# Filter pass: attention output matmuls in four row groups, column differences on GpSimd

## What is computed

```python
def _conv_att2(x, kg_w1, kg_b1, kg_w2, kg_b2, lk_filter, fus_w, fus_b):
    f_att, f_idt = (x[:, :ATT], x[:, ATT:])
    ...
    out_dk = jax.vmap(dyn)(f_att, ker)
    out_lk = _conv(f_att, lk_filter, pad=LK // 2)
    out = jnp.concatenate([out_lk + out_dk, f_idt], axis=1)
    return _conv1x1(out, fus_w, fus_b)
...
x = x + _L0_conv_ref(_gn(x), ...)
x = x + _L1_conv_ref(_gn(x), ...)
```

## Time and profile before

| | us |
|---|---|
| median of 3 runs | 2881.2 (2880.36 to 2883.96) |
| profiled execution, span from first to last instruction | 2878.9 |
| PE matmul busy | 2655.4 (92%) |
| VectorE busy | 2144.7 (74%) |
| ScalarE busy | 1055.2 (37%) |
| GpSimd busy | 639.2 (22%) |

### The profile page before, as it was taken

One profiled execution on the slowest core, in us unless ns is written; L12 is line 12 of the kernel. 1 busy time (PEld: TensorE's weight loads), 2 busy tenths in 40 slices (PEclk: granted clock), 3 DMA queues, 4 the chain that ended last, 5 costly groups with the idle time before them and its releaser, 6 DMA issues. The chain is left out here.

```text
span 2878.9 us, 38918 instructions
## 1 busy us (share of the span) xinstructions
PE 2655.4 (92%) x12262; PEld 2134.0 (74%) x12262; DVE 2144.7 (74%) x2968; ACT 1055.2 (37%) x1641; POOL 639.2 (22%) x663
## 2 busy tenths in 40 slices
PE   5999999979998899999998799999967999999998
PEld 4777777758887688888886677777745777777776
DVE  5444444554554888888887799999878999999998
ACT  0211111111110788988997322222103233233232
POOL 6544444312221444444443100000001000000000
PEclk9999999978896899999999899999978999999999
DMA  7222222210000887787775133334442343333332
GB/s 149 68 77 75 75 76 75 54 34 6 13 13 18 196 224 218 219 220 216 221 214 166 62 134 135 135 135 155 156 155 108 97 122 92 98 118 93 98 119 59
DMA packets 288703, 338.04 MB, mean 117 GB/s; under 512 B 24817, under 2 KB 243825, under 8 KB 274289
## 3 DMA queue, kind: packets, MB, share of 16 engines
q1 hardware_dynamic: 280736, 334.74, 39.6%
q10 hardware_dynamic: 7888, 2.29, 0.5%
HBM read 211.60 MB, written 122.62 MB: 116 GB/s over the span
## 5 line engine op out<-in xcount | busy, mean ns | idle before, releaser
L168 PE MATMUL ps_all<-vh,u_h 128*128 128x512 f32 x960 | 384.9, 401 | 28.3 <-DVE vl L2819 27.3
L170 PE MATMUL ps_all<-vh,u_l 128*128 128x512 f32 x960 | 383.6, 400 | 0.0
L169 PE MATMUL ps_all<-vl,u_h 128*128 128x512 f32 x960 | 383.2, 399 | 0.0
L2728 ACT ACTIVATE vh<-rt,gn 128x528 fp32r<-128x528 f32 x192 | 130.4, 727 | 446.1 <-DVE rt L2796 314.7
L168 PE MATMUL ps_all<-vh,t_h 128*128 128x512 f32 x576 | 231.6, 402 | 23.4 <-DVE vl L1874 23.3
L168 PEld LDWEIGHTS ps_all<-vh,u_h 128*128 128x128 f32 x960 | 181.0, 189 | 81.8 <-issue 34.8
L169 PE MATMUL ps_all<-vl,t_h 128*128 128x512 f32 x576 | 230.1, 399 | 0.0
L170 PE MATMUL ps_all<-vh,t_l 128*128 128x512 f32 x576 | 229.4, 398 | 0.0
L170 PEld LDWEIGHTS ps_all<-vh,u_l 128*128 128x128 f32 x960 | 181.1, 189 | 46.3
L169 PEld LDWEIGHTS ps_all<-vl,u_h 128*128 128x128 f32 x960 | 181.3, 189 | 45.6
L1713 POOL TENSOR_TENSOR zr<-zr,z 128x256 f32<-128x256 f32 x128 | 122.5, 976 | 343.4 <-DMA xr<-in_x 343.4
(11 more groups left out here) (401 smaller groups left out, 6760.0 us busy)
## 6 DMA issues: line engine op xcount, KB each, us to landing
xr<-in_x SPq DMA_DIRECT2D x128, 256.0 KB, 3.6
x_layer<-xr SPq DMA_DIRECT2D x64, 512.0 KB, 2.7
xq<-x_layer SPq DMA_DIRECT2D x32, 1024.0 KB, 4.9
x_layer<-xq SPq DMA_DIRECT2D x32, 1024.0 KB, 3.8
out<-ot SPq DMA_DIRECT2D x64, 512.0 KB, 5.2
xw<-in_x SPq DMA_DIRECT2D x112, 288.0 KB, 4.3
xc<-in_x SPq DMA_DIRECT2D x120, 256.0 KB, 3.9
xw<-x_layer SPq DMA_DIRECT2D x16, 1152.0 KB, 8.7
```

What stands on the lines that cost most here:

```text
L168: pe.matmul(o, wh, xh, start=first, stop=False, skip_group_check=True)
L169: pe.matmul(o, wh, xl, start=False, stop=False, skip_group_check=True)
L170: return pe.matmul(o, wl, xh, start=False, stop=last, skip_group_check=True)
L2728: act.activation(vh[:, v % 2, n, :, :].rearrange("p a b -> p (a b)"), rt[:, n, :, :].rearrange("p a b -> p (a b)"), ACT.Identity, scale=gn ...
```

## The change

Three edits, all for the filter pass:

1. `slot` becomes dc * 2 + dr, so the two pixels of one dc lie in 32 partitions side by side, from 32 * dc.
2. `attention` multiplies for each dc only those 32 partitions: 12 matmuls as before, but of 32 rows, in the order pass by pass, the four dc inside. It waits for all four banks to be free at once, and the four are full in the last pass.
3. `raw` and `differences` are issued by GpSimd, with a `period` of its own: raw 8 of the image before, then raw 1, raw 2, the two differences, raw 4, 5 and 7. Their waits are as before. `high` and `low` are unchanged and wait for the same semaphores.

```diff
--- before.py
+++ after.py
@@ -43,7 +43,7 @@
 
 def slot(dr, dc):
 
-    return (dc // 2) * 4 + dr * 2 + dc % 2
+    return dc * 2 + dr
 
 
 def par(r):
@@ -2147,6 +2147,43 @@
                     b_g.done(pool.tensor_tensor(ga_l[:, :, :], gf, ga_h[:, :, :].bitcast(F32), ALU.subtract))
                     assert b_g.n == NBG
 
+                    def raw(n, k):
+                        m = 6 * n + 2 * (k // 3) + k % 3
+                        if not (isinstance(m, int) and m < 3):
+                            pool.wait_ge(v_l, 9 * n + (k - 2 if k > 2 else 0))
+                        if k == 1:
+                            pool.wait_ge(xp_f, 16 * (n + 1))
+                        v = {1: (fx[:, 2, :, 0:8], fx[:, 3, :, 0:8]), 2: (fx[:, 3, :, 0:8], fx[:, 0, :, 1:9]),
+                             4: (ea[:, 0, :, 0:8], ea[:, 1, :, 0:8]), 5: (ea[:, 1, :, 0:8], eb[:, 0, :, :]),
+                             7: (eb[:, 0, :, :], eb[:, 1, :, :]), 8: (eb[:, 1, :, :], ea[:, 0, :, 1:9])}[k]
+                        if k > 3:
+                            pool.wait_ge(e_d, 2 * n + 2)
+                        pool.tensor_tensor(rw[:, k % 3 - 1, :, :], v[0], v[1], ALU.subtract).then_inc(r_d, 1)
+                    def differences(n, first):
+                        if not first:
+                            pool.wait_ge(v_l, 9 * n)
+                        pool.wait_ge(xp_f, 16 * (n + 1))
+                        pool.tensor_tensor(ea[:, :, :, :], fx[:, 0:2, :, :], fx[:, 2:4, :, :], ALU.subtract).then_inc(e_d, 1)
+                        pool.tensor_tensor(eb[:, :, :, :], fx[:, 2:4, :, 0:8], fx[:, 0:2, :, 1:9],
+                                          ALU.subtract).then_inc(e_d, 1)
+                    def period(i, a, s, n):
+                        if i is not None:
+                            raw(i, 8)
+                        if n is not None:
+                            raw(n, 1)
+                            raw(n, 2)
+                            differences(n, i is None)
+                            for k in (4, 5, 7):
+                                raw(n, k)
+                    b_s.at(pool, 0, NBS)
+                    pool.wait_ge(b_p, 4)
+                    schedule(pool, period)
                 @block.scalar
                 def _(act):
                     def high(n, k, first):
@@ -2241,29 +2278,6 @@
 
                 @block.vector
                 def _(dve):
...
                     def low(n, k):
                         src = rw[:, k % 3 - 1, :, :] if k % 3 else (fx[:, 3, :, 0:8], ea[:, 1, :, 0:8], eb[:, 1, :, :])[k // 3]
                         dve.wait_ge(v_h, 9 * n + k + 1)
@@ -2416,8 +2430,6 @@
 
                     def period(i, a, s, n):
                         first = i is None
-                        if i is not None:
-                            raw(i, 8)
                         if a is not None:
                             outputs(a, 2)
                         if i is not None:
@@ -2429,7 +2441,6 @@
                         if a is not None:
                             low_lk(a, 0)
                         if n is not None:
-                            raw(n, 1)
                             dynamic_taps(n, first)
                             low(n, 1)
                         if s is not None:
@@ -2437,7 +2448,6 @@
                         if i is not None:
                             outputs(i, 0)
                         if n is not None:
-                            raw(n, 2)
                             dynamic_sums(n, 0, first)
                         if s is not None:
                             variance(s)
@@ -2451,17 +2461,13 @@
                         if a is not None:
                             low_lk(a, 1)
                         if n is not None:
-                            differences(n, first)
                             low(n, 3)
-                            raw(n, 4)
                         if a is not None:
                             add_attention(a, 1)
                         if n is not None:
                             low(n, 4)
                         if a is not None:
                             low_lk(a, 2)
-                        if n is not None:
-                            raw(n, 5)
                         if s is not None:
                             edges(s)
                         if a is not None:
@@ -2476,7 +2482,6 @@
                         if a is not None:
                             add_attention(a, 2)
                         if n is not None:
-                            raw(n, 7)
                             dynamic_sums(n, 2, first)
                         if a is not None:
                             add_attention(a, 3)
@@ -2541,11 +2546,17 @@
                         mm.then_inc(main, 1)
 
                     def attention(a, c):
                         pe.wait_ge(l_l, 4 * a + c + 1)
-                        for dc in range(4):
-                            pe.wait_ge(qfree, 16 * a + 4 * c + dc + 1)
-                            product(pe, ps_all[:, 3 + dc, :], ga_h[:, dc, :], ga_l[:, dc, :], lh[:, c % 2, :],
-                                    ll[:, c % 2, :], True, True).then_inc(qful, 1)
+                        pe.wait_ge(qfree, 16 * a + 4 * c + 4)
+                        for w, v, first, last in ((ga_h, lh, True, False), (ga_h, ll, False, False),
+                                                  (ga_l, lh, False, True)):
+                            for dc in range(4):
+                                rows = slice(32 * dc, 32 * dc + 32)
+                                mm = pe.matmul(ps_all[:, 3 + dc, :], w[rows, dc, :], v[rows, c % 2, :], start=first,
+                                               stop=last, skip_group_check=True)
+                                if last:
+                                    mm.then_inc(qful, 1)
 
                     def border(s):
 
```

More of the change, by code:

```diff
@@ L2243, in _ @@
                 def _(dve):
[L2244 to L2265, removed]
                     def low(n, k):
```

## The result

The changed kernel takes 2884.0 us (median of 20 runs, 2876.63 to 2889.17), the kernel before 2879.8 (20 runs, 2874.63 to 2883.96): a ratio of 1.0013 with the interval [1.0007, 1.0019], so 3.7 us more, between 2.0 and 5.5. (Where this document gives a ratio, differences are taken from it; it is not the quotient of the two medians, which are 4.2 apart here.) That is slower, but by less than the 5.8 us that count here as no change, and by less than a third of the 13 forecast. 2884 lies inside the range; what was wrong is the size.

The account below looks back on a forecast made before the run. DVE was taken to bound the six periods in which all parts run. Four full periods +10, the two before them +1.6, first period +6 and the end -4.5 made +13.1, so 2894 us, range 2866 to 2916.

Parts of the forecast that it names:

- The bound: Filter pass: DVE bounds the six periods in which all parts run, PE having about 6 us to spare per period.
- DVE held by GpSimd: Full periods: DVE instructions reading two SBUF operands wait out GpSimd's instructions, costing 9.1 us of DVE time each period.
- Attention in row groups: PE's attention chunk: 1.4 us instead of 2.8, 5.6 us less per image, worth nothing while DVE is the bound.
- the wait before add_attention(1): DVE in a full period: new wait of 0.8 us, since all four banks become full only in the last set.
- the last two periods: End of the pass, without a next image: four shorter chunks give 5.6 back, less 1.1 for late banks, -4.5 us.
- First period: Start of the pass: DVE reaches the first dynamic weights 7 us later, PE has little slack, +6 us.
- the two after them: Two periods before the four full ones at +2.5 each: +1.1 and about +0.5, together +1.6 us.
- A: Rival: DVE isn't held by GpSimd, full periods give -6.6 us, total 2836 us; chance 0.08.
- D: Rival: GpSimd is slower on rows of 8 elements, 1.8 us per small subtraction, total 2913 us; chance 0.12.
- C: Rival: PE doesn't run the four groups side by side, a chunk takes 3.1 us, total 2905 us; chance 0.08.
- B: Rival: the turns fall better, 2.8 of the 9.1 us go, total 2881 us, or about 2870; chance 0.17.
- 0.55 for 2884 to 2904: Chance of the forecast case; its ends are the 9.1 us price off by 1.1 and the first period by 3.

Follow-up runs that it names:

- row groups alone: Kernel before plus only the new slot and attention in 32-row groups, raw and differences staying on DVE: 2873.1 us beside 2880.6, ratio 0.9977.
- kernel with placed subtractions: Changed kernel with raw 1 and 2 back on DVE and GpSimd's other subtractions started at add_attention's first bank reads: 2855.6 us beside 2880.6, ratio 0.9916.
- doubled work: Changed kernel with every GpSimd subtraction done twice into the same place: 2948.3 us beside 2878.9, ratio 1.0236.
- kernel without the first burst: Changed kernel with the first image's raw 1 to 7 and differences back on DVE: 2880.4 us beside 2878.9, ratio 1.0003.
- kernel without row groups: GpSimd's subtractions started beside PSUM reads, raw 1 and 2 on DVE, but attention and slot as before the change: 2870.1 us beside 2878.9, ratio 0.9970.

## Why the prediction came out too high

**The bound: right.** DVE binds the full periods; with PE 7% less busy (row groups alone, 56.5 us a period instead of 61.0) three of the four stayed at 64.7, and the fourth came down to it.

**DVE held by GpSimd: right in kind, and nearly in size.** Predicted 9.1 us a period, measured 8.4. The price of GpSimd's own instructions was right (1.20 to 1.30 us for a small one, forecast 1.3; `ea` 2.90 undisturbed, forecast 2.85; `eb` 2.17, forecast 2.55), and so was the list of who is held: low_lk 1.2 (measured 1.17), first tap step 2.6 (2.67), tiny subtraction 1.0 (1.01). `eb` was to hold the multiply for 1.8 and held it for 1.25, since 1.2 of its 2.6 us pass while the tap step finishes and the reduce runs. raw 5 was to cost 0.4 and cost 0.5, raw 7 0.9 (0.8), raw 8 0.9 (1.0). The rule of the Trainium skill (SBUF — State Buffer, "SBUF: two separate sides"), an exclusive lock for the whole instruction, fits: 1.17 us for one element. The kernel with placed subtractions shows nothing held where DVE reads PSUM or takes its statistics. That one operand is always safe doesn't follow: with doubled work the copy of one SBUF operand went from 0.17 to 0.96.

**Attention in row groups: the term was mis-sized.** I had 1.4 us for a chunk, from pairs of 64 rows. Timeline of PE in the changed kernel:

```profile
1814.88 0.51 PE L2556 MATMUL ps_all<-lh,ga_h 32*128 32x512 f32 x4 [3.29 <-DVE ll L2360]
1815.21 0.40 PE L2556 MATMUL ps_all<-ll,ga_h 32*128 32x512 f32 x4
1815.44 0.41 PE L2556 MATMUL ps_all<-lh,ga_l 32*128 32x512 f32 x4
1815.78 0.44 PE L2569 MATMUL ps_all<-rowf,row_w 64*64 64x128 f32 x4
```

Four start together, the sets are 0.33, 0.23 and 0.34 apart: 0.90 us instead of 2.80, 3.1 times as fast. The second set starts after the same 0.23 as a single matmul of 128 rows; the 0.10 that I added for weights fell on the first alone, so the reading of the earlier trace rows behind it, that weights of the same row group are not loaded under a running matmul, doesn't carry over to these. The Trainium skill (TensorE: Matmul & The Clock Gate, "Measured speedup vs the span model") has 3.07 times, from which the prediction had derived this very 0.9 and set it aside for the row. It doesn't change the full periods, but two terms: the wait before add_attention(1) is 0.47 to 0.89, 0.67 on average, and not 0.8, and the last two periods gain 4 x 1.9 - 1.1 = 6.5 instead of 4.5. Measured: from the last low(n, 0) to `neg` 166.3 instead of 170.5, -4.2, of which the one full period in it is some +1.6 (by the others), so the end about -5.8 by estimate.

**First period: the step that failed.** Forecast +6, measured -0.2 for the first two periods together (66.5 us after, 66.7 before), and 1.3 by the kernel without the first burst. The delay itself came: the first dynamic weights are there 13.9 us after the first low instead of 8.0, 5.9 later (forecast 7). But the step from there, "PE starts its dynamic taps that much later and has little slack", was read from a busy share and not from PE's waits, and it is what failed: the delay hardly reaches the length of the two periods. These are waits of PE around the first two periods, 1575 to 1665, before:

```profile
PE ps_all L168 <- ACT cc L2174: 4.8, 1, 4.8
...
PE ps_all L168 <- DVE w_l L2317: 3.3, 1, 3.3
```

and after:

```profile
PE ps_all L168 <- DVE w_l L2331: 10.3, 1, 10.3
```

PE waits 7.0 us more for the weights and 4.8 us less for ACT's copy, which before was late for component 3. That leaves 2.2 of the delay, and the granted clock takes them up. Busy time from first to third low(n, 0), and six microseconds behind the wait for the copy, before:

```profile
1595.62:1662.28 66.66, 57.56 (x221) 45.77 (x222) 50.12 (x74) 20.47 (x32) 0.00 (x0) 0.88 0.19 68
...
1622.00:1628.00 6.00, 4.61 (x11) 3.71 (x12) 5.93 (x11) 1.83 (x3) 0.00 (x0) 0.50 0.00 0
```

and after:

```profile
1590.65:1657.12 66.47, 54.91 (x218) 43.71 (x219) 53.77 (x58) 19.57 (x32) 31.34 (x17) 0.87 0.19 68
```

Before, PE stood still for 4.8 us and then ran at the lower level (0.50 of full speed, 1.2 GHz) for some 6 us; after, its slow stretch lay behind the longer wait for the weights (0.50 from 1605 to 1611 us), and from 1614 us on it was at 1.00 throughout. It is busy 2.7 us less for the same work. So +7.0 - 4.8 - 2.7 = -0.5, and -0.2 was measured. The wait for the copy and the slow stretch behind it were as good as slack. With GpSimd's work doubled the first two periods take 82.5 us, 16 more than in the changed kernel: PE waits 5.2 us more for the weights and 9.1 us for the copy again, since that is late as well. A later input of PE is absorbed only as long as the others aren't delayed with it.

**The sum again, with measured terms:** first two periods -0.2 (forecast +6); the two after them +0.5 and -0.4 (+1.6; the second of these was 67.1 long before, lengthened by the low clock and the wait named above, so these two say little); three full ones +4.8 (+7.5); the last full one and the end -4.2 (-2). In all +0.5 in the profiled pair and +3.7 by the ratio of the runs. The forecast was 13.1, so of an error of 12.6 us in the pair the first period makes 6.2, the periods after it 4.2 and the end 2.2. Why the runs show 3.7 and the pair 0.5 stays open in part: the kernel before is on record in one profile, and had its period of 67.1 taken 64.7 like the others, the pair would be at +2.9.

**Rivals.** A (DVE not held) is out. D (GpSimd slow on rows of 8) too: 560 elements in rows of 8 took 1.20 to 1.30 us. C (groups not side by side) is out. B, about even, came nearest in its number (2881) but not for its reason: the turns fell as forecast. Of the 0.55 for 2884 to 2904 the result hit the very edge; that it lies inside is luck. No errors cancelled: first period, full periods and end were each forecast too slow.

## What to carry to other kernels

Work moved from DVE to GpSimd isn't free because GpSimd is idle: list which DVE instructions run beside each moved one, charge a full GpSimd instruction to each that reads two operands from SBUF, and start the moved ones beside instructions that the rows show unheld: here the reads of PSUM, the statistics and the reduce, but not a copy within SBUF. Here that made 26 us of difference between two kernels, measured side by side, that differ in where GpSimd starts and in two small subtractions. Before a delay is counted in the sum, follow the delayed engine to its next wait for someone else: that wait absorbs it first, as long as what it waits for isn't delayed too. Look also at the granted clock behind each of the two waits.

## What the runs showed that I had not expected

- Four 32-row matmuls of 512 columns in separate row groups start every 0.23 us as a set, the same pitch as one full matmul, after a first set of 0.33.
- A DVE instruction on one element per partition pays the whole remaining GpSimd instruction: 0.16 became 1.17 us, and 2.50 on average with doubled work.
- A copy of one SBUF operand was held as well: 0.17 us became 0.96 beside a doubled GpSimd subtraction.
- With less to do PE was granted a lower clock: 0.92 in a full period with row groups alone against 0.97 before (rows below, before first). Where DVE binds, that costs nothing (64.70 us both times); where PE binds, a clock of 0.97 and 0.95 instead of 1.00 goes with periods 2.7 and 3.8 us longer (rows of the kernel without row groups above).

```profile
1792.60:1857.30 64.70, 60.95 (x282) 48.64 (x281) 61.10 (x94) 17.26 (x24) 0.00 (x0) 0.97 0.40 150
...
1783.90:1848.60 64.70, 56.48 (x282) 43.69 (x281) 61.01 (x94) 17.30 (x24) 0.00 (x0) 0.92 0.40 150
```
